# Expert affinities as eight extra columns of the value and output projections, and routing three steps behind attention

## The reference, cut to what matters

```python
x = L0_attn_x                                    # (16, 256, 128) float32
x = x + layernorm(attention(layernorm(x), WQ, WK, WV, WO))     # 16 heads of 8, causal
x = x + layernorm(moe(layernorm(x), centroids, ln_g, ln_b, w1, b1, w2, b2))

def moe(x, ...):                                 # 4096 tokens, 8 experts, hidden 512
    aff = x @ centroids.T                        # (4096, 8)
    assign = argmax(aff, axis=1)                 # each token goes to one expert
    alpha = sigmoid(aff of the chosen expert)
    ye = x + relu(layernorm_e(x) @ w1[e].T + b1[e]) @ w2[e].T + b2[e]
    return alpha * ye + (1 - alpha) * x
```

## Time and profile before

| | us |
|---|---|
| median of 3 runs | 408.97 (408.82 to 411.0) |
| the profiled execution, its own time | 409.43 |
| its span, first to last instruction | 407.7 |
| PE busy | 330.6 (81%) |
| DVE busy | 327.9 (80%) |
| ACT busy | 236.9 (58%) |
| POOL busy | 239.6 (59%) |
| PE's idle time ahead of the first scores, up to 25.65, ended by the load of the queries and keys | 7.04 |

### The profile page before, as it was taken

How to read it: one execution, slowest core, us unless ns; L and a number is a source line. 1 busy time by engine, 2 the same in 40 slices (tenths; PEclk the granted TensorE clock), 3 DMA queues, 4 the chain that set the end, 5 groups by cost and what they waited for, 6 DMA issues and landing times.

```text
span 407.7 us, 11164 instructions
## 1 busy us (share of the span) xinstructions
PE 330.6 (81%) x3642; PEld 265.4 (65%) x3642; DVE 327.9 (80%) x1215; ACT 236.9 (58%) x574; POOL 239.6 (59%) x321
## 2 busy tenths in 40 slices
PE   2447979999999999999999998988415999899940
PEld 1225667776776777776777776755314999899930
DVE  7846789969889889898898898777660999899980
ACT  2202567576576675684774864655204788788940
POOL 4831364565385585674664766558360388788883
PEclk9998999999999999999999999999555999999985
DMA  7563574664553544625535537012036667767600
GB/s 219 109 114 52 91 171 89 90 121 89 82 104 74 91 94 53 114 75 73 110 71 80 116 71 102 21 41 67 16 95 161 180 174 189 201 171 196 193 30 6
DMA packets 34680, 42.78 MB, mean 105 GB/s; under 512 B 5465, under 2 KB 25053, under 8 KB 33088
## 3 DMA queue, kind: packets, MB, share of 16 engines
q1 hardware_dynamic: 31744, 37.43, 45.0%
q0 software_dynamic: 2304, 4.37, 3.2%
q10 hardware_dynamic: 576, 0.27, 0.3%
HBM read 30.59 MB, written 11.66 MB: 104 GB/s over the span
## 4 chain that ended last, share of the span: by engine, by line
PE 42%; DVE 17%; issue 11%; DMA 11%; ACT 9%; POOL 8%; SPq 1%; POOLq 0%; DVEq 0%; ACTq 0%
PE O L871 6%; PE S L837 5%; PE ST L850 3%; DMA aug<-nmT 3%; DVE nmf L1113 3%; PE S L832 3%; PE MB L797 3%; ACT p L609 3%; POOL out_x L540 3%; PE O L875 2%; DMA w1s<-in_w1x 2%; DMA aug<-qk_parts 2%; PE MB L885 2%; POOL xs_rows L473 2%; ACT xn L659 2%
## 5 line engine op out<-in xcount | busy, mean ns | idle before, releaser
L1113 DVE TENSOR_REDUCE nmf<-S 128x2 f32<-128x512 f32 (+1 forms) x192 | 129.6, 682 | 33.9 <-PE S L837 25.5
L609 ACT ACTIVATE p<-ST 128x1024 f32<-128x1024 f32 x64 | 65.5, 1023 | 30.6 <-PE ST L850 30.5
L453 POOL TENSOR_SCALAR_AFFINE_SELECT p<-p 128x512 f32<-128x512 f32 x64 | 40.7, 636 | 52.6 <-ACT p L613 52.0
L449 POOL TENSOR_SCALAR_AFFINE_SELECT p<-p 128x512 f32<-128x512 f32 x64 | 40.5, 633 | 31.1 <-ACT p L609 30.8
L837 PE MATMUL S<-aug 126*128 126x128 bf16 x512 | 50.7, 221 | 0.0
L540 POOL DMA_INDIRECT out_x<-vaug,x_all x39 | 42.4, 1087 | 7.9 <-issue 7.9
L837 PEld LDWEIGHTS S<-aug 126*128 126x128 bf16 x512 | 40.3, 99 | 3.7
L832 PE MATMUL S<-causal,identb 128*128 128x256 bf16 x128 | 35.9, 281 | 7.6 <-DVE nmf L1113 7.2
L850 PE MATMUL ST<-aug 128*128 128x256 bf16 x256 | 38.5, 272 | 3.9 <-DMA aug<-nmT 2.6
L871 PE MATMUL O<-p,vaug 128*32 128x256 f32 x512 | 41.1, 390 | 0.5 <-POOL p L449 0.5
L613 ACT ACTIVATE p<-ST 128x512 f32<-128x512 f32 x64 | 38.8, 606 | 0.0
(11 more groups left out here) (162 smaller groups left out, 862.2 us busy)
## 6 DMA issues: line engine op xcount, KB each, us to landing
w1s<-in_w1x SPq DMA_DIRECT2D x39, 259.0 KB, 3.2
qk_parts<-qkp SPq DMA_DIRECT2D x16, 384.0 KB, 3.3
aug<-qk_parts SPq DMA_DIRECT2D x32, 192.0 KB
aug<-qk_parts SPq DMA_DIRECT2D x32, 128.0 KB
x_all<-xs_rows SPq DMA_DIRECT2D x39, 67.0 KB, 2.2
aug<-qk_parts SPq DMA_DIRECT2D x32, 64.0 KB
w_tab<-in_w2t SPq DMA_DIRECT2D x8, 256.0 KB
out_x<-vaug,x_all POOLq DMA_INDIRECT x39, 3.0
```

Of the source, the lines that this page charges most:

```text
L449: g.affine_select(out=v, in_=v, compare_op=ALU.is_ge, fill=0.0, base=0, pattern=[[0, 4], [1, P]], channel_multiplier=-1).then_inc(s["sel0" ...
L453: g.affine_select(out=v, in_=v, compare_op=ALU.is_ge, fill=0.0, base=0, pattern=[[0, 4], [1, P]], channel_multiplier=-1).then_inc(s["sel1" ...
L609: a.activation(p0[:, gr % 2], ST0[:, :, :], ACT.Exp, scale=SCALE).then_inc(s["exp0"], 1)
L1113: v.tensor_reduce(dst, S[:, n % 2].rearrange("p (j n) -> p j n", j=k), op=ALU.max, axis=AX_X, negate=True).then_inc(s["red"], 1)
```

## The change

The centred centroids become eight more columns of the value weights (`wat[:, 2, D:D + E]`), so the value projection of a batch gives, beside the values, the dot products of the normalised x with the centroids. Multiplied by the standard deviation of x (`sdx`, made once by `deviation`) they are the part of the affinity that comes from x; ACT stores them in `xc` in `v_out`, with two scaled copies a batch. The product of the output weights with the centred centroids becomes eight more columns of `wo`, so the output projection gives the part from the attention, which goes through `yb`. DVE adds the two with two `scalar_tensor_tensor` of eight columns in the new function `affinities`. The transpose of x2, its copy `fT`, the product with `centc` and the copy to `aff` are gone. Affinities are there in step t-2, so that the choice moves from t-3 to t-2, and ranks, positions, gates and scatters from t-4 to t-3; there are 19 steps in place of 20.

At the start the centroids are loaded ahead of the rest of x, and batch 0's value projection stands behind the centroids' sums, thus behind the transposes and projections of batches 0 to 2. The transposed output weights `woT` are loaded in step 0, and `centroid_weights` and `keep_centroid_weights` run in step 1.

```diff
-            for i in range(B + 4):
+            for i in range(B + 3):
@@ ACT, v_out
+                act.wait_ge(s["sd_x"], group(b) + 1)
+                src = MB[:, 0:2 * (D + E)].rearrange("p (t n) -> p t n", t=2)
+                for t in (0, 1):
+                    a.activation(xc[:, b.times(2, t)], src[:, t, D:D + E], ACT.Identity, scale=b.pick(sdx, 1, 2, t))
@@ ACT, y_out
-                a.activation(yb[:, i.slot(RING)], MA[:, 0:SEQ].rearrange("p (t d) -> p t d", t=2), ACT.Copy).then_inc(s["y_d"], 1)
-
-            def fT_out(i):
...
+                a.activation(yb[:, i.slot(RING)], MA[:, 0:2 * (D + E)].rearrange("p (t d) -> p t d", t=2), ACT.Copy).then_inc(s["y_d"], 1)
+
+            def ranks_out(i):
+                act.wait_ge(s["rk_r"], i.times(1, 1))
+                a.activation(i.pick(rank, 2, 2), MB[:, 0:2 * E].rearrange("p (t e) -> p t e", e=E), ACT.Copy).then_inc(s["rk_d"], 1)
@@ ACT, step: exp_negative moves from behind exp_far(t, 3) to behind shift_out(nxt, 0)
+                if l3:
+                    exp_negative(l3)
@@ PE, project_v
-                    last = mm(MB[:, t * P:(t + 1) * P], xnT[:, b.slot(RING), t * P:(t + 1) * P], wat[:, 2],
+                    last = mm(MB[:, t * (D + E):(t + 1) * (D + E)], xnT[:, b.slot(RING), t * P:(t + 1) * P], wat[:, 2],
@@ PE, step
-                    if gr == 1 and (ln or last):
-                        affinities_and_ranks(i.plus(-3), ln, last)
+                    if gr == 1 and l3:
+                        ranks(l3)
...
-                    if gr == 0 and ln:
-                        transpose_f(ln)
@@ DVE
+            def affinities(b):
+
+                dve.wait_ge(s["v_d"], b.times(1, 1))
+                for t in (0, 1):
+                    last = v.scalar_tensor_tensor(out=aff[:, b.times(2, t)], in0=yb[:, b.slot(RING), t, D:D + E],
+                                                  scalar=rs_y[:, t:t + 1], in1=xc[:, b.times(2, t)], op0=ALU.mult, op1=ALU.add)
+                last.then_inc(s["af_d"], 1)
@@ POOL, step: the scatters are those of l3, and the second stands behind the power
-                if last:
-                    scatter(last, 1)
-                if ln and t:
-                    power(ln, 1)
+                if l2 and t:
+                    power(l2, 1)
+                if l3:
+                    scatter(l3, 1)
```

More of the change, by code:

```diff
@@ L231, in sandwich_kernel, with group @@
         LAST = B - 1
+        def group(b):
+            return next(n for n, (lo, hi) in enumerate(STATS) if lo <= 2 * b.k < hi)
         def x_row(b, t):
@@ L510, in step @@
             def step(i):
-                t, new, ln, last = at(i, 0), at(i, 3), at(i, -2), at(i, -4)
+                t, new, l2, l3 = at(i, 0), at(i, 3), at(i, -2), at(i, -3)
                 if t:
@@ L514, in step @@
                     select(t, 1)
-                if ln:
-                    power(ln, 0)
-                if ln and not t:
-                    power(ln, 1)
+                if l2:
+                    power(l2, 0)
+                if l2 and not t:
+                    power(l2, 1)
                 if t:
                     select(t, 2)
-                if last:
-                    scatter(last, 0)
+                if l3:
+                    scatter(l3, 0)
                 if new:
@@ L652, in normalise_x @@
             def normalise_x(b):
-                n = next(n for n, (lo, hi) in enumerate(STATS) if lo <= 2 * b.k < hi)
-                act.wait_ge(s["nb_x"], n - 1)
+                act.wait_ge(s["nb_x"], group(b) - 1)
                 act.wait_ge(s["xnT_r"], b.times(1, 1 - RING))
@@ L675, in step @@
             def step(i):
-                t, new, nxt, old, l2, ln, last = (at(i, n) for n in (0, 3, 1, -1, -2, -3, -4))
+                t, new, nxt, old, l2, l3 = (at(i, n) for n in (0, 3, 1, -1, -2, -3))
                 if t:
@@ L685, in step @@
                     o_out(old)
[L686 to L687 removed]
                 if t:
                     exp_near(t, 1)
[L690 to L691 removed]
+                if l3:
+                    ranks_out(l3)
                 if new:
@@ L1301, in _ @@
             x_bias(2)
+            deviation(2)
             def step(i):
-                new, nxt, old = at(i, 3), at(i, 1), at(i, -1)
-                l2, l3, l4 = at(i, -2), at(i, -3), at(i, -4)
+                new, nxt, old, l2, l3 = (at(i, n) for n in (3, 1, -1, -2, -3))
                 if nxt:
```

178 lines of the change are left out of this document (82 added, 96 removed).

## The result

The changed kernel takes 405.41 us (median of 4 runs, 403.5 to 410.5), the kernel before 409.86 beside it; the ratio is 0.9886, 95% interval 0.9844 to 0.9928. Run twice more, among the experiments, the changed kernel took 408.78 us, ratio 0.9932 (0.9895 to 0.9969), and 405.49, 0.9888 (0.9857 to 0.992). So it gains 0.7 to 1.1%, some 3 to 5 us, where 12 were forecast. The profiled execution took 405.06, its span is 403.3.

A forecast was written before the change was run, and what follows sets the result against it. A step was taken as a loop of PE's and DVE's halves, neither alone setting it. Gains of 6.75 (steps 3 to 11), 1.8 (12 to 14) and 3.4 (end) make 12.0 us: 397 us, range 393 to 402.5.

The forecast's parts named there:

- The step: Full attention step: PE loses 0.82 us of work, less 0.1 on DVE; 0.75 taken, from 15.82 to 15.05 us.
- the times nine: Steps 3 to 11 of the attention: each gains 0.75 us, 6.75 in all.
- As long as DVE's waits there last: Groups 0 and 1: PE's savings shorten the step one for one while DVE's waits, 1.91 us in all, cover them.
- The cover is used up; each further 0.1 us on ACT would cost the step 0.1.: Two scaled copies on ACT delay masks by 0.4 us; group 0's far mask ends at 183.04, its product starts at 183.0.
- The sum: Gain of a full step: 0.82 less 0.1, thus 0.72, taken as 0.75 us; steps 12 to 14 give 1.8 together.
- The end: Last batch's routing and scatters after the steps: 3.4 us earlier.
- its two halves: At the end: 0.85 us earlier last power, and 2.5 us from four scatters instead of six behind it.
- The start: Centroid sums and batch 0's value projection hide in PE's 7.04 us wait; without that cover, 2 us once.
- the load of `woT` replaces that of the centroids: At the start, one load takes the other's place; no cost was counted.
- DVE's half: DVE's operations in a step: 0.27 + 0.16 - 0.07 - 0.36 = 0, plus 0.1 for `hotk` meeting POOL's operation.
- the port rule: DVE operations reading two SBUF tiles wait for POOL's; behind (1,0) up to 2 x 0.6 us, just hidden.
- The rivals: DVE waiting longer for POOL: 402 (0.27) or 412.6 (0.08); DVE gaining too: 393.5 (0.12); end not shorter: 399.5 (0.05).

The follow-up runs named there:

- half the bytes: Six loads of the parts cut from 768 to 384 KB a step, in both kernels; steps 3 to 11 take 135.1 us changed, 142.3 before.
- the swap on ACT: Changed kernel with ACT's last exponential of a step ahead of its copies of the values (xc, vaug); 398.84 and 399.32 us. In the kernel before: ratio 1.0002.
- the run with the columns alone: Changed kernel with affinities as eight more columns, but routing still four steps behind in the old order, 20 steps; 405.3 us, ratio 0.9866.
- without scatters: Changed kernel with all 32 scatters moved out of the steps to the end of the attention; only steps 3 to 11 read, 136.0 us.

## Why the prediction was wrong

- **The step was right, the times nine was wrong.** "As long as DVE's waits there last" was the only condition on the 0.75 us. Its terms hold: an undisturbed step is 0.86 shorter, and nine of them with half the bytes give 7.2. What failed is that only engines were asked whether they would be late. The small load had 6.33 us between issue and need before (187.05 to 193.38), and after 82.92 no wait stood at it; that did not mean that it had room. The load doesn't follow its own issue: it lands with the last of the 768 KB, 9.9 to 11.0 us after the first of them was issued before and 10.2 to 13.0 after. A step 0.86 shorter takes 1.1 us from the time in which they must land (150.24 to 161.75 before, 149.65 to 160.03 after), and 10.4 us is no longer enough. Steps 3 to 11 gained 3.1 for 6.75: 3.6 of the missing 7.6 us are this, in the two other profiles of the kernel 5.4 and 5.2. That the swap on ACT makes the transfers land sooner, though all but the scatter are issued and needed as before, stays unexplained.
- **"The cover is used up; each further 0.1 us on ACT would cost the step 0.1."** The sum priced this at nothing, and in steps 12 to 14 at nothing too. That step failed: there ACT's new copies put POOL's power and scatter on the chain. 1.6 us were missing, and the swap brings all of it back.
- **The end** was forecast at 3.4 and measured at 3.0; its two halves, 0.85 and 2.5, are 1.0 and 2.0 by the run with the columns alone. (The first half has a slip: 0.71 and 0.42 are 1.13, not 1.15.)
- **The start** was called hidden and cost 1.7 us; "the load of `woT` replaces that of the centroids" overlooked that PE now needs it in group 1 of step 1 (it waited 0.45), and DVE's copy behind it (0.56). Loading it early takes these waits away; how much of the rest is DVE's added work was not taken apart. With half the bytes the cost is 3.2 (80.08 and 83.26).
- **DVE's half and the port rule.** The sum of 0 holds. The Trainium skill, SBUF — State Buffer, "Who interferes with whom", speaks of operations with two SBUF inputs, and these paid nothing behind (1,0) in the undisturbed step. The same section names `tensor_scalar` among the operations that can enter a two-port mode and then contend with GpSimd as well; the prediction left that out. `ve_y` (L1187 above) is such an operation, with one input, and took 0.94 while POOL masked. The trace agrees with a wait for POOL; in which mode the operation ran no run shows. With the swap it took 0.16 in every step of both profiles, and an undisturbed step 14.89 for 14.96. In steps 13 and 14 `x_all`, with two inputs, took 1.03 for 0.60 beside a mask.
- **The rivals.** None came true. All spoke of engines; one that says "a transfer has less time than it needs, lost: its lateness times the steps" was missing, and it would have named the largest part of what was lost.

## What to carry to other kernels

When a loop gets shorter, list for every transfer in it the time from its issue to its first use, before and after, beside the bytes that land in that time, and count from the first issue of everything in flight ahead of it, not from its own; a load that causes no wait now may have no room. And read the order of work on an engine beside a wait (here a copy with slack ahead of an exponential without) before calling its new work hidden: swapping the two was worth more than the change. Where steps of one profile differ while those before were alike to 0.01 us, take a second profile before explaining any one step.

## What the runs showed of the hardware

- A wait of PE can cost more than itself. In the steps, waits of 1.80, 2.00 and 2.33 us were each followed by some 3 us at a granted clock of 0.50, waits of 1.62 and 1.75 us were not; nor were waits of 2.03 us (kernel before, 53.96) and 2.28 us (without scatters, 54.06) at the start of the loop. The length of the wait alone does not decide it.
- An 8 KB load issued with 768 KB in flight ahead of it lands with the last of them, 9.6 to 13.0 us after their first issue, whether it stands in their queue or in ACT's. Where PE waited for it on their queue, that was 6.0 to 8.5 us after its own issue. With 384 KB ahead it lands 1.9 to 2.0 us after its own issue.
- Issuing one such load from ACT in a step costs the step 0.2 us (15.20 for 14.96, 16.00 for 15.82).
